# First layer of a four-layer conv kernel: maximum scores from the high parts in 32-row tiles, second head group projected between the first maxima, ones written a batch ahead

## What is computed

```python
tokens = x.reshape(B, C, N).transpose(0, 2, 1)          # B=8, C=256, N=1024
qkv = (tokens @ w_proj + b_proj).reshape(B, N, 8, 96)    # 8 heads, 32 columns each of q, k, v
q, k, v = jnp.split(qkv, 3, axis=-1)
attn = softmax(einsum('bihd,bjhd->bijh', q, k) * 32**-0.5, axis=2)
res = einsum('bijh,bjhd->bihd', attn, v).reshape(B, N, 256)
out = res @ w_out + b_out + tokens
```

## Time and profile before

| | |
|---|---|
| median of three runs | 3214.05 (3213.63 to 3219.43) |
| profiled execution, span from first to last instruction | 3214.9 |
| TensorE matmul busy | 85% |
| VectorE busy | 69% |
| ScalarE busy | 38% |
| GpSimd busy | 20% |
| mean granted TensorE clock | 0.924 |

### The profile page before, as it was taken

How to read it: one execution, slowest core, us unless ns; L and a number is a source line. 1 busy time by engine, 2 the same in 40 slices (tenths; PEclk the granted TensorE clock), 3 DMA queues, 4 the chain that set the end, 5 groups by cost and what they waited for, 6 DMA issues and landing times.

```text
span 3214.9 us, 45307 instructions
## 1 busy us (share of the span) xinstructions
PE 2731.7 (85%) x16502; PEld 1884.4 (59%) x16502; DVE 2212.3 (69%) x2474; ACT 1234.2 (38%) x1348; POOL 657.1 (20%) x397
## 2 busy tenths in 40 slices
PE   5889969899798897988879888798887998878983
PEld 4447754577545774457744677447764477644772
DVE  4766668666686675866668666785677756777666
ACT  2443325433254332543335333353333533244333
POOL 0430115201061021500225002340024300243011
PEclk8989989999899998999989999899988999889996
DMA  6100050000500004000040000400022000310015
GB/s 152 23 24 1 1 120 6 24 1 14 113 1 24 1 14 113 1 24 1 14 112 1 24 1 32 95 1 24 1 64 62 24 1 1 92 35 24 1 53 235
DMA packets 46400, 124.77 MB, mean 39 GB/s; under 512 B 9792, under 2 KB 21312, under 8 KB 42560
## 3 DMA queue, kind: packets, MB, share of 16 engines
q1 hardware_dynamic: 46144, 121.41, 14.1%
HBM read 43.01 MB, written 23.86 MB: 21 GB/s over the span
## 4 chain that ended last, share of the span: by engine, by line
PE 65%; DVE 12%; issue 9%; SPq 4%; DMA 4%; ACT 4%; DVEq 0%; ACTq 0%
PE tile L1264 22%; PE pv L1264 10%; PE tile L1358 8%; PE pv L1374 6%; PE tile L1336 5%; DVE small L871 4%; PE tile L1518 4%; SPq L445 4%; PE tile L1395 3%; DMA stack<-ones 2%; PE tile L1540 2%; PE tile L1648 1%; PE tile L1567 1%; PE tile L1417 1%; DMA stack<-qk_r 1%
## 5 line engine op out<-in xcount | busy, mean ns | idle before, releaser
L871 DVE TENSOR_REDUCE small<-tile 128x1 f32<-128x1024 f32 x512 | 610.6, 1219 | 210.9 <-PE tile L1336 210.1
L660 ACT ACTIVATE p<-tile 128x1024 f32<-128x1024 f32 x512 | 520.9, 1023 | 568.9 <-PE tile L1358 564.5
L1358 PE MATMUL tile<-stack 112*128 112x512 f32 x1024 | 387.0, 462 | 129.5 <-DMA stack<-ones 87.8
L547 POOL TENSOR_TENSOR acc<-acc,p 128x1024 f32<-128x1024 f32 x160 | 397.6, 2505 | 176.9 <-DVE acc L903 175.0
L1264 PE MATMUL tile<-qk_r 128*128 128x512 f32 x1536 | 378.0, 395 | 0.0
L1336 PE MATMUL tile<-stack 96*128 96x512 f32 x1024 | 339.8, 424 | 34.9 <-DMA stack<-qk_r 31.0
L1358 PEld LDWEIGHTS tile<-stack 112*128 112x128 f32 x1024 | 162.9, 196 | 350.7 <-issue 227.5
L572 POOL TENSOR_TENSOR row_sum<-act 128x256 f32<-128x256 f32 x32 | 42.1, 1335 | 1488.9 <-DVE act L1099 1488.9
L1374 PE MATMUL pv<-p,v 128*32 128x256 f32 (+1 forms) x3584 | 321.2, 431 | 9.4 <-ACT p L660 7.6
L1264 PEld LDWEIGHTS tile<-qk_r 128*128 128x128 f32 x1536 | 287.1, 188 | 66.6 <-issue 7.7
L1104 DVE TENSOR_TENSOR pl<-p,ph 128x1024 fp32r<-128x1024 f32 x128 | 158.2, 1236 | 238.2 <-ACT p L745 238.2
(11 more groups left out here) (277 smaller groups left out, 4356.9 us busy)
## 6 DMA issues: line engine op xcount, KB each, us to landing
stack<-qk_r SPq DMA_DIRECT2D x192, 256.0 KB, 5.0
x_in<-in_x_dram SPq DMA_DIRECT2D x9, 1024.0 KB, 7.6
act<-in_x_dram SPq DMA_DIRECT2D x8, 1024.0 KB, 11.0
x_scratch<-act SPq DMA_DIRECT2D x7, 1024.0 KB, 3.9
z_scratch<-zbuf SPq DMA_DIRECT2D x7, 1024.0 KB, 5.1
stack<-ones SPq DMA_DIRECT2D x8, 512.0 KB, 10.1
w3f<-w3f_scratch SPq DMA_DIRECT2D x8, 512.0 KB, 3.3
fin_rest<-z_scratch SPq DMA_DIRECT2D x3, 1024.0 KB, 12.6
```

Source lines behind the costliest of these rows:

```text
L547: pe.tensor_tensor(total, first, p0[:, jt % DEPTH, pair, :], ALU.add).then_inc(pool_done, gps.one("add0", *u, jt, pair))
L660: sc.activation(p0[:, jt % DEPTH, pair, :], tile_wait(b, "st0", *u, jt, pair), ACT.Exp, scale=float(D) ** -0.5).then_inc(scalar_done, scal ...
L871: ve.tensor_reduce(maxima[:, h * NT + it:h * NT + it + 1], t[:], X, ALU.max).then_inc(vector_done, vector.one("max0", g, h, it))
L1358: ins = mm(o[:, halves[k]], stack[0:K0, 1, g, h, jt * P:(jt + 1) * P], stack[0:K0, 0, g, h, halves[half]], start=True, stop=True)
```

## The change

Three edits. `s0` multiplies only the 32 rows of the high parts, for two heads at once: the two heads' rows lie at different multiples of 32 (`part_rows` swaps the first two parts for odd heads), each head has its own half of the tile, and a tile now covers half of the columns j of two heads (`s`). `max0` therefore gives two numbers a tile, and a new step `top0` takes the larger of the two column halves. The first unit's `s0` reads `qk_r` directly and does not wait for `stack`; `st0` takes over the wait. Group 1's projections move between the first unit's maxima, at the places in `BETWEEN`, and the projections of `v0` move behind them. The ones are written once ahead of the loop, and then at the end of each batch but the last, behind the step `g` of layer four. `win` shares memory with `rec0`, and `small` grows from 128 to 192 columns, to make room.

```diff
 def rows_of(unit, k):
     g, half = unit
-    h, t = divmod(k, HT)
-    return g, h, HT * half + t
+    pair, k = divmod(k, G * HT // 2)
+    s, t = divmod(k, HT)
+    return g, pair, s, HT * half + t
+def part_rows(h, k):
+    return D * ((h % 2, 1 - h % 2, 2)[k])
+BETWEEN = {3: ("qk0", 0, 1), 6: ("qk0", 1, 1), 8: ("v0", 0), 10: ("v0", 1), 12: ("v0", 2), 14: ("v0", 3)}
...
-        maxima = small[:, 0:G * NT]
...
+        maxima = small[:, 0:64].rearrange("p (h t s) -> p h t s", h=G, s=2)
+        top = small[:, 64:96].rearrange("p (h t) -> p h t", h=G)
...
+            def key_ones():
+                sp.dma_start(stack[IMAX:K0, 1].rearrange("p g h (a n) -> p (g h a) n", n=P).bitcast(F32),
+                             ones[0:NMAX, :].rearrange("p (a n) -> p a n", a=1)
+                             .broadcast_to((NMAX, NG * G * N // P, P))).then_inc(key_ones_in, 16)
+            sp.wait_ge(vector_done, vector.count)
+            key_ones()
...
-                            sp.dma_start(stack[D * k:D * k + D, :, g, h, :].bitcast(F32),
+                            to = part_rows(h, k)
+                            sp.dma_start(stack[to:to + D, :, g, h, :].bitcast(F32),
...
-                sp.dma_start(stack[IMAX:K0, 1]...        .then_inc(key_ones_in, 16)
...
                 sp.dma_start(x3_dram[b], act[:]).then_inc(x3_stored, 16)
+                sp.wait_ge(tensor_done, tensor.at(b, "g"))
+                key_ones()
...
-                def max0(g, h, it):
-                    t = tile_wait("s0", g, h, it)
-                    ve.tensor_reduce(maxima[:, h * NT + it:h * NT + it + 1], t[:], X, ALU.max
+                def max0(g, pair, s, it):
+                    t = tile_wait("s0", g, pair, s, it)
+                    ve.tensor_reduce(maxima[:, 2 * pair:2 * pair + 2, it, s], t[:].rearrange("p (h n) -> p h n", h=2),
+                                     X, ALU.max
...
-                    negate((g, half), G, ts, ("max0", *rows_of((g, half), G * HT - 1)))
+                    own("max0", *rows_of((g, half), G * HT - 1))
+                    TT(top[:, :, ts], maxima[:, :, ts, 0], maxima[:, :, ts, 1], ALU.max
+                       ).then_inc(vector_done, vector.one("top0", g, half))
+                    negate((g, half), G, ts, ("top0", g, half))
...
-                def s0(g, h, it):
-                    if it == 0 or it == HT:
-                        pe.wait_ge(stacked[g][h], 48 * b + 48)
-                    o = free("s0", g, h, it)
-                    for s in halves:
-                        ins = mm(o[:, s], stack[0:IMAX, 0, g, h, it * P:(it + 1) * P], stack[0:IMAX, 1, g, h, s],
-                                 start=True, stop=True)
+                def s0(g, pair, s, it):
+                    unit = (g, it // HT)
+                    if unit == UNITS[0] and pair == 0 and s == 0 and it == 0:
+                        scalar_wait("qk0_hi", 1, g)
+                    o = free("s0", g, pair, s, it)
+                    for k in range(2):
+                        h = 2 * pair + k
+                        if unit == UNITS[0]:
+                            q, kk = (qk_r[D * h:D * h + D, t, 0, g] for t in range(2))
+                        else:
+                            if s == 0 and it == HT * unit[1]:
+                                pe.wait_ge(stacked[g][h], 48 * b + 48)
+                            first = part_rows(h, 0)
+                            q, kk = (stack[first:first + D, t, g, h] for t in range(2))
+                        ins = mm(o[:, halves[k]], q[:, it * P:(it + 1) * P], kk[:, halves[s]], start=True, stop=True)
...
                         if jt == 0:
+                            if (g, half) == UNITS[0]:
+                                pe.wait_ge(stacked[g][h], 48 * b + 48)
                             vector_wait("max_rows", g, half, h)
```

More of the change, by code:

```diff
@@ L73, in rows_of @@
     g, half = unit
-    h, t = divmod(k, HT)
-    return g, h, HT * half + t
+    pair, k = divmod(k, G * HT // 2)
[4 more added lines that the diff above has]
+BETWEEN = {3: ("qk0", 0, 1), 6: ("qk0", 1, 1), 8: ("v0", 0), 10: ("v0", 1), 12: ("v0", 2), 14: ("v0", 3)}
 def tensor_steps():
-    s = [("qk0", t, g) for g in range(NG) for t in range(2)]
+    s = [("qk0", t, 0) for t in range(2)]
     for k in range(G * HT):
-        s += [("v0", k // 3 - 1)] if k in (3, 6, 9, 12) else []
+        s += [BETWEEN[k]] if k in BETWEEN else []
         s += [("s0", *rows_of(UNITS[0], k))]
@@ L139, in vector_steps @@
 def vector_steps():
-    s = [("qk0_lo", t, g) for g in range(NG) for t in range(2)]
-    s += [("max0", *rows_of(UNITS[0], k)) for k in range(G * HT)]
-    s += [(n, 0, 0) for n in ("neg_hi", "neg_copy", "neg_lo")] + [("max_rows", 0, 0, h) for h in range(G)]
+    s = [("qk0_lo", t, 0) for t in range(2)]
+    for k in range(G * HT):
+        s += [("qk0_lo", *BETWEEN[k][1:])] if k in BETWEEN and BETWEEN[k][0] == "qk0" else []
+        s += [("max0", *rows_of(UNITS[0], k))]
+    s += [(n, 0, 0) for n in ("top0", "neg_hi", "neg_copy", "neg_lo")] + [("max_rows", 0, 0, h) for h in range(G)]
     for u in UNITS:
@@ L153, in vector_steps @@
         if following:
-            s += [(n, *following) for n in ("neg_hi", "neg_copy", "neg_lo")]
+            s += [(n, *following) for n in ("top0", "neg_hi", "neg_copy", "neg_lo")]
             s += [("max_rows", *following, h) for h in range(G)]
@@ L311, in conv_seq_kernel @@
         pool_w = sb("pool_w", [P, POOLED, POOLED])
-        small = sb("small", [P, 128])
+        small = sb("small", [P, 192])
         max_in = sb("max_in", [P, N], F32R)
@@ L382, in conv_seq_kernel @@
         logits, mix_e, logits_in = pairs[:, 32:36], pairs[:, 36:40], pairs[:, 40:44]
-        win = sb("win", [P, NT * C // WIN])
         win_r = sb("win_r", [P, NT * C // WIN])
@@ L958, in aggregate @@
                         ve.bn_aggr(mv[:, ct, :], stats[:, ct]).then_inc(vector_done, vector.one("mv", layer, ct))
-                for g in range(NG):
-                    for t in range(2):
-                        if g == 0 and t == 1:
-                            dve.wait_ge(z_stored, 16 * b)
-                            dve.wait_ge(x3_stored, 16 * b)
-                            dve.wait_ge(pool_done, gps.before(b, "pool", 9, CT - 1))
-                        qk0_lo(t, g)
+                qk0_lo(0, 0)
+                dve.wait_ge(z_stored, 16 * b)
+                dve.wait_ge(x3_stored, 16 * b)
+                dve.wait_ge(pool_done, gps.before(b, "pool", 9, CT - 1))
+                qk0_lo(1, 0)
                 for k in range(G * HT):
+                    if k in BETWEEN and BETWEEN[k][0] == "qk0":
+                        qk0_lo(*BETWEEN[k][1:])
                     max0(*rows_of(UNITS[0], k))
@@ L1423, in _ @@
                 pe.wait_ge(vector_done, vector.before(b, "x_lo", CT - 1))
-                for g in range(NG):
-                    for t in range(2):
-                        qk0(t, g)
+                for t in range(2):
+                    qk0(t, 0)
                 def v0_tile(k):
@@ L1436, in _ @@
                 for k in range(G * HT):
-                    if k in (3, 6, 9, 12):
-                        v0_tile(k // 3 - 1)
+                    if k in BETWEEN:
+                        {"qk0": qk0, "v0": v0_tile}[BETWEEN[k][0]](*BETWEEN[k][1:])
                     s0(*rows_of(UNITS[0], k))
```

20 lines of the change are left out of this document (9 added, 11 removed).

## The result

| kernel | median | range | ratio to before, 95% |
|---|---|---|---|
| before | 3213.84 | 3212.02 to 3219.43 | |
| after | 3353.64 | 3330.57 to 3363.31 | 1.0412 [1.0387, 1.0437] |

The medians alone give a ratio of 1.0435. Kernels with much half clock in their loops vary more from one execution to the next (same_rows, further down, by 65 in 3509), and all medians here are over all executions.

The account below looks back on a forecast made before the run. It took SyncE's queue and the transfers to bound the head of the layer, TensorE the loop within units. From 3214, -44 (head) + 7 (`top0`) + 7 (loop) = -30 gave 3184, its own range 3170 to 3203, overall 3150 to 3214.

Parts of the forecast that it names:

- the loop's term: Loops of three of four units: rounds of 1.745 for 1.71, nine of 16 counting, +7 us in all.
- `exp0` 5.5 earlier, -44 in eight: Head of the batch: the first `exp0` at 478.1 instead of 483.58, 5.5 us a batch, 44 in eight.
- Half clock throughout: Head's worst clock case: both moved projections at half clock, `exp0` at 478.9, a gain of 4.7 a batch, 37 in all.
- VectorE's gaps: Head: VectorE idle ahead of `qk0_lo(0, 1)` and `(1, 1)`, 1.7 us at full clock or 4.1 at half.
- Transfers decide, by 1 us.: Head: the stack transfers land at 478, the maxima's path is ready at 477, so transfers set the first `exp0`.
- `top0`, +7: From the last maximum to `m0` in all four units: one more small instruction of 0.21 us, +7 in all.
- A round of 1.68 to 1.79: Loop: one round of `st0`, `s0` and `pv0` takes 1.68 to 1.79 us after the change, for 1.71 before.
- my two cases for the second head: Loop's `s0`: the other head's matmul comes at the same time (0) or after its own weights (0.11).
- Slower: Rival, 0.08: dearer shape switches in the loop, at 2.0 a round +63, total 3240; decides from 1.88 a round on.
- Clock or tiles help: Rival, 0.22: full clock at the head (-58), the loop gains (-28), or both; 3135 to 3170.
- The loop takes it back: Rival, 0.10: the two heads run one after the other, 1.91 a round; total 3220, or 3208 to 3220 partly absorbed.
- My fourth rival: Rival, 0.10: transfers past 463 and maxima past 478, so `exp0` moves only 2 to 3 us; 3208.

Follow-up runs that it names:

- same_rows: The changed kernel with the high parts of both heads in the same 32 rows, so their tiles can't run at once; 3509.17, ratio 1.0865.
- loop_only: The changed kernel with the head of the batch as before the change, keeping 32-row tiles in the loops; 3421.35, ratio 1.0650.
- rows96: The changed kernel with 96 rows instead of 32 in the loops' `s0`, two heads still together in a tile; 3176.14, ratio 0.9868.
- ones_early: The kernel before with only the third edit, the ones written ahead of the loop and then behind step `g`; 3146.79, ratio 0.9784.
- head_proj_first: The changed kernel with the loops as before the change and group 1's projections again ahead of all maxima; 3147.51, ratio 0.9791.
- rows64: The changed kernel with 64 rows of each head in the loops' scores, one head after the other; 3322.66, ratio 1.0319.
- rows66: The changed kernel with 66 rows of each head in the loops' scores, the full array's shape; 3270.42 over four executions, ratio 1.0143.
- both_rows: The changed kernel with both heads' 96-row products added in the loops ahead of the 32-row ones, which overwrite them; 3412.04, ratio 1.0609.

## Why the prediction was wrong

**The step that failed** is the loop's term, "9 x 0.035 = 0.3 a unit, x 24 units = +7". Its rounds were right and its clock was not. I priced a round from rows at 1.00 and asked about the clock only in the head, where TensorE waits. That the clock could be at half in a stretch where TensorE is busy throughout stood in no term and in no rival. The term measured about +197 (202 of half clock, less 5), and loop_only, which has it without the head, gives the same: 3421.35 - 3217.25 = 204, less 7 for `top0`. rows96 takes it away. Why the clock falls there stays open beyond what the experiments above say.

**By its own steps:**

- *`exp0` 5.5 earlier, -44 in eight.* Right in kind, mis-sized: 8.6 in this batch (40.5 - 31.9), 54 in sum. I had group 1's low parts at +17.4 from SyncE's first issue, behind group 0's last, and so a gap. They ended at 465.21 - 450.61 = +14.6, in time for SyncE's 24 issues to run through in 28.30. "Half clock throughout" was too dark: the first moved projection has its matmuls at 1.22 for two at 451.77 and at 0.68 at 454.49, and the second ran full. VectorE's gaps were 3.30 and 1.97, for 4.1 and 4.1 at worst.
- *But the moved projections did not earn this.* ones_early and head_proj_first have 32 to 33 in all batches with the projections first. Where they are between the maxima, some batches have 36.8 and some 22 us of half clock in the head; rows96 has four such batches and one at 34.8. That and `top0` are 21 + 7 = 28 of the 42 between the profiled executions of rows96 (span 3186.9) and ones_early (3144.5). The medians of the two differ by 29.
- *"Transfers decide, by 1 us."* Right that they decide. Maxima ended 26.9 after the first issue, 3.3 earlier than I had them (473.3 - 443.1 = 30.2), and `exp0` follows the last landing (477.56 + 4.78).
- *`top0`, +7.* Right: 477.73 - 477.52 = 0.21.
- *A round of 1.68 to 1.79.* At full clock 1.67, just under the lower end, with the pieces as worked out: 0.67 to `s0`, 0.43 to `pv0`, 0.57 to `st0`. Of my two cases for the second head, the lower was right: in the trace's records its matmul starts 2 ns behind the first head's (both at 908.11), where in same_rows it starts 0.34 behind. So 1.68 was the better choice than 1.745. The Trainium skill (TensorEngine Tiling (Array Packing), Key Properties) says that a change of mode drains TensorE; the trace agrees: from `st0`'s first matmul to `s0`'s it is 0.67, for 0.58 with 96 rows (530.86 - 530.28), and so the halved array time went into the switches.

**The rivals.** "Slower" had the right sign with the wrong mechanism: it needed a round of 1.88 from dearer switches, and at full clock the switch cost what the forecast had it cost. What decided was a round of 2.89 from the clock. "Clock or tiles help" was right about the head's clock in most batches; the loop outweighed it. "The loop takes it back" through heads that run one after the other did not occur in the changed kernel. same_rows does run them so (a round of 1.89, near the 1.91 of that rival), and at 3509.17 it is slower again by its clock; rows64 runs them so too, and with less half clock it is quicker than the changed kernel (3322.66). My fourth rival, late transfers and late maxima, did not occur either (`exp0` 8.6 earlier).

The Trainium skill (TensorE: Matmul & The Clock Gate, Part 1) puts a half clock down to idle stretches of TensorE, and by it these loops would run full. The trace disagrees: 44.00 busy of 44.00 at 0.50, and the waits ahead of the falls are 0.6 to 1.5 long, about as long as the 1.00 that the kernel before has at full clock. The measurement decides.

## What to carry to other kernels

A TensorE step that is made smaller, by fewer rows or by tiles of another shape, may cost a whole loop its clock, though TensorE hardly waits in it; so price such a change at both clocks and compare the granted clock of the loop before looking at anything else. An untouched instruction that gets slower (`st0`, 462 to 554 ns) is the quickest sign of it. And test the edits of a change one by one: here one of three, the ones written a batch ahead, gave a gain of about 67, and the other two together cost 207 (3353.64 - 3146.79).

## What the hardware showed that I had not expected

- Half clock (1.2 GHz, where full is 2.4) with TensorE busy without a gap: 40.00 of 40.00 at 0.50 in loop_only, 50.00 of 50.00 in same_rows.
- The same loop at either clock, mostly by the clock it started with: rows66 3262.21 (median of three), and 3160.80 with 21 filler matmuls, 15 ahead of the loop and 6 behind its second `st0`.
- More TensorE time in a round is no remedy by itself: same_rows and both_rows add some and have 3509.17 and 3412.04. (both_rows does get most of its clock back: half clock is 224 over its eight batches for 555 in the changed kernel, but a round at full clock takes 2.13 for 1.67.)
- Two 32-row tiles at different rows do run side by side: the pair of 512-column matmuls took 0.50, where the pair in same_rows, both in rows 0 to 31, took 0.73. Each loads its own weights, and two switches stand around them, so the round fell by 0.04 only.
